# Rotary embedding in an attention stage: the swap as an f32 matmul, the projection copied out by ScalarE, cosine on GpSimd, sine on VectorE

## The reference

```python
def _rotate_half(x):
    x1, x2 = jnp.split(x, 2, axis=-1)
    return jnp.concatenate([-x2, x1], axis=-1)

def _apply_rope(x, cos, sin):
    return x * cos + _rotate_half(x) * sin

q = (x @ Wq).reshape(Bd, Sd, H, DH + D_ROPE)        # x: (4, 512, 256), H = 16, DH = 16, D_ROPE = 64
q_nope, q_rope = (q[..., :DH], q[..., DH:])
c_kv = x @ Wdkv
kv = (c_kv @ Wukv).reshape(Bd, Sd, H, 2 * DH)
k_rope = x @ Wkr
q_rope = _apply_rope(q_rope, cos, sin)
k_rope = _apply_rope(k_rope, cos, sin)
scores = einsum(q_nope, k_nope) + einsum(q_rope, k_rope)
attn = softmax(where(causal, scores * scale, -1e9))
out = einsum(attn, v).reshape(Bd, Sd, H * DH) @ Wo
```

## Time and profile before

| | us |
|---|---|
| median of three runs | 1441.34 |
| lowest, highest | 1438.83, 1446.45 |
| the profiled execution | 1443.96 |
| its span, first to last instruction | 1442.2 |

### The profile page before, as it was taken

How to read it: one execution, slowest core, us unless ns; L and a number is a source line. 1 busy time by engine, 2 the same in 40 slices (tenths; PEclk the granted TensorE clock), 3 DMA queues, 4 the chain that set the end, 5 groups by cost and what they waited for, 6 DMA issues and landing times. The chain is left out here.

```text
span 1442.2 us, 32153 instructions
## 1 busy us (share of the span) xinstructions
PE 1169.6 (81%) x12288; PEld 881.9 (61%) x12288; DVE 985.1 (68%) x2082; ACT 647.3 (45%) x1519; POOL 599.3 (42%) x525
## 2 busy tenths in 40 slices
PE   2789898998874599998817885998999648999992
PEld 1356566665653398987713553665766527989882
DVE  6479798887786556456565956788797574555554
ACT  4367566666564133333446653353333223333342
POOL 0245445545430234334300195688696213333220
PEclk9899999999995599999958998999999759999996
DMA  4655756656533598876240002000000039966635
GB/s 158 155 131 157 175 167 172 167 164 158 147 111 87 197 419 345 277 248 252 66 173 8 15 25 45 16 17 2 2 2 2 27 93 397 419 238 243 253 99 186
DMA packets 98186, 216.83 MB, mean 150 GB/s; under 512 B 28977, under 2 KB 68146, under 8 KB 91890
## 3 DMA queue, kind: packets, MB, share of 16 engines
q1 hardware_dynamic: 88434, 192.22, 41.0%
q0 software_dynamic: 7488, 20.46, 4.2%
q10 hardware_dynamic: 2112, 2.10, 0.4%
HBM read 157.40 MB, written 40.04 MB: 137 GB/s over the span
## 5 line engine op out<-in xcount | busy, mean ns | idle before, releaser
L1228 ACT ACTIVATE ffn_h<-ffn_bank,ffn_b 128x256 f32<-128x256 f32 (+1 forms) x384 | 143.9, 431 | 278.5 <-PE ffn_bank L118 259.3
L1407 DVE CAST ffn_hh<-ffn_h 128x512 f16<-128x512 f32 (+1 forms) x192 | 80.7, 420 | 182.8 <-ACT ffn_h L1228 166.5
L116 PE MATMUL ffn_bank<-ffn_hh,ffn_W 128*128 128x256 f16 (+1 forms) x768 | 181.0, 254 | 8.9 <-DVE ffn_hl L1409 8.9
L1042 POOL DMA_INDIRECT ffn_xs<-xn_rows,ffn_from_rows x78 | 79.4, 1019 | 244.4 <-PE ffn_bank L1123 158.2
L118 PE MATMUL ffn_bank<-ffn_hh,ffn_W 128*128 128x256 f16 (+1 forms) x768 | 180.8, 254 | 0.0
L117 PE MATMUL ffn_bank<-ffn_hl,ffn_W 128*128 128x256 f16 (+1 forms) x768 | 180.7, 253 | 0.0
L644 ACT ACTIVATE att_prob<-att_bank,att_nmax 128x512 f32<-128x512 f32 (+3 forms) x256 | 127.1, 525 | 31.3 <-DVE att_nmax L726 30.0
L733 DVE TENSOR_TENSOR att_ptl<-att_bank,att_pth 128x384 f16<-128x384 f32 (+1 forms) x192 | 113.9, 593 | 34.4 <-ACT att_pth L651 34.4
L651 ACT ACTIVATE att_pth<-att_bank 128x384 f16<-128x384 f32 (+1 forms) x192 | 101.3, 528 | 79.0 <-PE att_bank L591 79.0
L1049 POOL DMA_INDIRECT y_rows<-ffn_y,ffn_to_rows x78 | 77.4, 993 | 133.6 <-DVE ffn_y L1418 86.9
L591 PE MATMUL att_bank<-main_identf,att_prob 128*128 128x128 f32 x640 | 99.6, 281 | 35.7 <-ACT att_prob L644 19.6
(11 more groups left out here) (345 smaller groups left out, 3222.6 us busy)
## 6 DMA issues: line engine op xcount, KB each, us to landing
ffn_W<-split_w SPq DMA_DIRECT2D x46, 2048.0 KB, 19.3
att_piece<-in_ffn_w SPq DMA_DIRECT2D x32, 512.0 KB, 5.2
split_w<-att_halves SPq DMA_DIRECT2D x32, 512.0 KB, 4.2
att_Q<-att_pair SPq DMA_DIRECT2D x64, 128.0 KB, 2.4
ffn_back<-y_rows SPq DMA_DIRECT2D x16, 512.0 KB, 9.1
att_KB<-att_krl SPq DMA_DIRECT2D x8, 512.0 KB, 5.6
att_Q<-att_pair SPq DMA_DIRECT2D x64, 64.0 KB, 2.1
xn_rows<-ffn_XN SPq DMA_DIRECT2D x8, 512.0 KB, 2.6
```

What stands on the lines that cost most here:

```text
L116: pe.matmul(out, ah, bh, start=start, stop=False)
L1228: ins_ = act.activation(h[layer][:, m, 0:n], bank[1 + 2 * layer + u][:, (m % 2) * n:(m % 2 + 1) * n], ACT.Gelu, bias=bias[:, ds(e + m, 1)])
```

## The change

The swapped weights `wt`, and the swapped columns of `wx`, are gone. A job's first half is as before. Its second half is two f32 matmuls on `turned`: a signed swap matrix (`swap`, made once by DVE from the identity) times the sine product, and the identity times the cosine product, added in bank 1. The products are now made from a copy `raw` of the projection in SBUF: ACT makes the copy, POOL the cosine product, DVE the sine product. ACT then reads bank 1 twice, for the f16 high part and for the f32 `rope`, from which POOL makes the low part as before. POOL's sum is gone. In the start, each job's first half is put ahead of the second half of the job before it.

```diff
+            def turn_half(job):
+                at = turn[job] % 2
+                pe.wait_ge(swap_made, 2)
+                pe.wait_ge(sin_done, turn[job] + 1)
+                pe.matmul(bank[1][:, :], swap[:, :], turned[:, at, 1, :], start=True, stop=False)
+                pe.wait_ge(cos_done, turn[job] + 1)
+                return pe.matmul(bank[1][:, :], identf[:, :], turned[:, at, 0, :], start=False, stop=True)
...
-                if what == "pair":
-                    ins = project(bank[1][:, :], wth, wtl, n % (NH // 2) * P, P, n // (NH // 2))
-                elif what == "kr":
-                    ins = project(bank[1][:, :], wxh, wxl, KT_AT, P, n)
+                if what in ("pair", "kr"):
+                    ins = turn_half(job)
...
-            for job in START:
-                first_half(job)
+            first_half(START[0])
+            for job, following in zip(START, START[1:] + [None]):
+                first_half(following)
                 second_half(job)
...
+            def copy_raw(job):
+                what, n = job
+                r = turn[job]
+                act.wait_ge(first_ready, nth[job] + 1)
+                if r >= 2:
+                    act.wait_ge(second_ready, nth_second[ropes[r - 2]] + 1)
+                act.activation(raw[:, r % 2, :], bank[0][:, :], ACT.Copy, scale=ATT_SCALE if what == "kr" else 1.0).then_inc(first_drained, 1)
...
-                act.wait_ge(summed, r + 1)
+                act.wait_ge(second_ready, nth_second[job] + 1)
...
-                    ins = act.activation(pair[:, n % 2, 0, :], rope[:, r % 2, :], ACT.Copy)
+                    ins = act.activation(pair[:, n % 2, 0, :], bank[1][:, :], ACT.Copy)
                 ins.then_inc(rope_high, 1)
+                if r >= 2:
+                    act.wait_ge(rope_low, r - 1)
+                act.activation(rope[:, r % 2, :], bank[1][:, :], ACT.Copy).then_inc(second_drained, 1)
...
+                if what in ("pair", "kr"):
+                    r = turn[job]
+                    dve.wait_ge(first_drained, nth[job] + 1)
+                    if r >= 2:
+                        dve.wait_ge(second_ready, nth_second[ropes[r - 2]] + 1)
+                    dve.tensor_tensor(turned[:, r % 2, 1, :], raw[:, r % 2, :], sinT[:, :], ALU.mult).then_inc(sin_done, 1)
+                    return
...
-                pool.tensor_tensor(rope[:, r % 2, :], turned[:, r % 2, 0, :], turned[:, r % 2, 1, :], ALU.add).then_inc(summed, 1)
+                    wait_alone(pool, second_ready, nth_second[ropes[r - 2]] + 1, passed)
+                pool.tensor_tensor(turned[:, r % 2, 0, :], raw[:, r % 2, :], cosT[:, :], ALU.mult).then_inc(cos_done, 1)
...
                 if last:
-                    sum_rope(last)
                     low_rope(last)
+                if job_at(g):
+                    cosine(job_at(g))
                 if g % 2 == 0:
                     high_piece(g // 2)
                     low_piece(g // 2)
```

More of the change, by code:

```diff
@@ L318, in attention_stage @@
         turned, rope = t.sb("turned", [P, 2, 2, S]), t.sb("rope", [P, 2, S])
-        pair = t.sb("pair", [P, 2, 2, S], F16)
+        pair, swap = t.sb("pair", [P, 2, 2, S], F16), t.sb("swap", [P, P])
+        raw = t.sb("raw", [P, 2, S])
         qnh, qnl, knh, knl = (t.sb(n, [P, 2, S], F16) for n in ("qnh", "qnl", "knh", "knl"))
@@ L367, in attention_stage @@
         nth_second = {job: n for n, job in enumerate(j for j in done if j[0] != "lat")}
-        turn = {job: n for n, job in enumerate(j for j in done if j[0] in ("pair", "kr"))}
+        ropes = [j for j in done if j[0] in ("pair", "kr")]
+        turn = {job: n for n, job in enumerate(ropes)}
         def wait_drained(eng, job):
@@ L655, in high_half @@
                 what, n = job
+                if what in ("pair", "kr"):
+                    high_rope(job) if x else copy_raw(job)
+                    return
                 if what not in ("lat", "qn", "kn", "v", "oT") or (what == "lat" and x):
@@ L693, in _ @@
                 high_half(job, 1)
-                high_rope(job)
             probs(0, 0)
@@ L717, in _ @@
         def _(dve):
+            halves_of = lambda a: a[:, :].rearrange("p (b x r) -> p b x r", x=2, r=HALF)
+            for x in range(2):
+                dve.tensor_scalar(halves_of(swap)[:, :, x, :], halves_of(identf)[:, :, 1 - x, :], -1.0, None, ALU.mult).then_inc(swap_made, 1)
             dve.memset(zeros[:, :], 0.0).then_inc(zeros_made, 1)
@@ L755, in drain @@
                 what, n = job
-                if what == "lat" and x:
+                if what in ("lat", "pair", "kr") and x:
                     return
-                if what in ("pair", "kr", "op"):
+                if what in ("pair", "kr"):
+                    r = turn[job]
[3 more added lines that the diff above has]
+                    dve.tensor_tensor(turned[:, r % 2, 1, :], raw[:, r % 2, :], sinT[:, :], ALU.mult).then_inc(sin_done, 1)
+                    return
+                if what == "op":
                     if x == 0:
@@ L826, in _, with cosine @@
         def _(pool):
-            def sum_rope(job):
+            def cosine(job):
                 what, n = job
@@ L843, in low_rope @@
                 wait_alone(pool, rope_high, r + 1, passed)
+                wait_alone(pool, second_drained, nth_second[job] + 1, passed)
                 if what == "kr":
@@ L864, in _ @@
             for job in START:
-                sum_rope(job)
+                cosine(job)
                 low_rope(job)
```

37 lines of the change are left out of this document (10 added, 27 removed).

## The result

| | before | after |
|---|---|---|
| median of four runs each, us | 1442.08 | 1563.57 |
| lowest, highest | 1438.83, 1446.45 | 1560.83, 1565.35 |
| span of the profiled execution | 1442.2 | 1563.6 |

The change makes the kernel slower by 121.5 us: a ratio of 1.084, interval 1.081 to 1.087. The direction was forecast, the size was not: 1478, with a range up to 1502.

What follows compares the result with a forecast made beforehand. PE and DVE were both taken as near their limit, so hand-overs count. Span 1442.2 + 30 (loop) + 2 (start) + 5 (clock) = 1479.2, put at 1478 us after adjusting from profiled span to median; range 1450 to 1502.

Steps and rivals of the forecast that it cites:

- Fewer weights: Before attention: the split of wt goes and wx shrinks, so attention starts about 2.4 us earlier.
- The chain up to the cosine: Even head: ACT's copy runs 115.62 to 116.22, POOL's cosine 116.40 to 117.67, and DVE's normalising product stands until 117.75.
- The rival without a lock: Even head: the sine runs beside the cosine, interval 11.84 us, kernel 1450 us; chance 0.15.
- The sine: Even head: DVE's sine product of 0.67 us follows the held normalising product and ends at about 118.36, not 117.69.
- The f32 matmul: PE, second half: 0.43 us each, two 0.86 against 1.29 for six fp16 matmuls; 15.5 us less PE work in all.
- The rival at four steps: PE, second half: each f32 job's half ends 0.86 us later, 26 us in all, kernel 1504 us; chance 0.03.
- The odd head: ACT's two copies ahead of chunk 1 make an odd head 5.67 us instead of 5.51, 0.15 more.
- The clock: Loop: low clock behind PE's new 1.7 us waits, +5 us net, ends 0 and +30.
- The rival by the clock: Loop: the clock falls at every PE wait, 36 us instead of 5, kernel 1509 us; chance 0.13.
- The start: Start of attention: later latent copy and longer key chain; +2 us with layer norm, ends 0 and +4.
- A gain taken for the change's: Loop: ACT's wait for POOL's sum, 20.8 us in 27 times, goes away; part of why intervals average 11.60, not 11.09.
- the interval of 11.09: Loop before the change: two heads between POOL's pair sums at 110.34 and 121.43; with +1.28 and +0.15 it becomes 12.52 us.

Runs made afterwards that it cites:

- piece_odd: The changed kernel with POOL's two passes over an expert piece moved from the even heads to the odd ones: 1548.28 us, 1.072 of the kernel before.
- sine_psum: The changed kernel with the sine product read from PSUM bank 0, still behind the normalising product: 1522.42 us, 1.058 of the kernel before.
- f16_swap: The changed kernel with the two products, swap matrix and identity of the second half in f16: 1518.91 us, 1.052 of the kernel before.
- sine_ahead: The changed kernel with the sine product read from PSUM bank 0 and placed ahead of the normalising product: 1491.65 us, 1.034 of the kernel before.
- start_order: The kernel before with only the new order of PE at the start of attention: 1455.20 us, 1.007 of the kernel before.
- old_start: The changed kernel with PE's order at the start of attention as it was before: 1555.28 us, 1.076 of the kernel before.
- f16_old_start: The changed kernel with f16 second-half matmuls, the sine from PSUM ahead of the normalising product, and the old start order: 1424.64 us, 0.991 of before.
- rope_last: The kernel before with ACT's high half of the rope sum moved behind the next head's second softmax piece: 1436.48 us, 0.994 of the kernel before.
- no_cosine: The changed kernel without POOL's cosine product, the identity matmul taking the raw copy: 1514.39 us, 1.049 of the kernel before.

## Why the prediction was wrong

By its own steps, on the head shown above:

- **Fewer weights: right.** -2.0 us against -2.4.
- **The chain up to the cosine: right.** Copy 3.19 and cosine 3.97 us behind the head's first transposes were forecast, 3.17 and 4.06 measured. The normalising product stands until 0.09 behind the cosine, as forecast. The rival without a lock is out.
- **The sine: the step that failed most.** "The sine product of 0.67" was taken to run once the cosine had ended. The prediction named what is queued behind the wait on DVE and on PE, but not what is queued behind the cosine on POOL: the cast, without a pause. At the cosine's end the normalising product is served, the cast has begun, and the sine has to wait for it (piece_odd and sine_psum show it). With that the sine took 1.52, and the swap starts 7.00 us into the head and not 6.00. 30 x 1.00 = 30 us.
- **The f32 matmul: mis-sized by half.** "Four such f32 matmuls ... 1.88" read the "x4" of the earlier trace rows as matmuls. It counts records, and an f32 matmul has two, so the row is two matmuls of 0.86. The job costs 1.72 instead of 0.86, more than the 1.29 of the six it replaces: PE loses 15.5 us where I let it gain as much. 30 x 0.86 = 26 us. The rival at four steps, to which I gave 0.03 against the page FP8 and Floating Point Precision of the Trainium skill (TensorE Precision Notes, 4 passes for true fp32), was the true case; f16_swap's trace agrees with the page, one fourth of the step in f16. The row never spoke against it.
- **The odd head: right.** 5.67 was forecast. The interval 133.66 to 148.86 less 9.38 leaves 5.82: 30 x 0.15 = 5 us.
- **The clock: too small.** Swap and identity are 1.72 of work by the steps and take 2.38 in the head shown (136.60 to 138.98), because the second half of them is at the low level behind the wait, like the 0.63 of L589 at 140.47: 0.66 a head, 20 us, where 5 was taken. The heads differ widely. Of the loop's 33 halves 14 take 1.79 or 1.80, the full clock, and 12 take 3.2 to 3.6, as here:

```profile
151.80 2.04 PE L516 MATMUL att_bank<-att_turned,att_swap 128*128 128x512 f32 x2 [2.31 <-DVE att_turned L786]
153.64 1.63 PE L518 MATMUL att_bank<-att_turned,main_identf 128*128 128x512 f32 x2
```

  The mean is 2.48, so that over all of them it is 25 us and not 20. The length of the wait alone does not decide: waits of 2.18 us had both outcomes (93.15 and 108.27), the three of 3.10 the slow one. In sine_ahead, with waits of 0.73 in the mean, none of the 33 takes over 1.8. The rival by the clock thus held in part.
- **The start: wrong cause and size.** +9.2 to the scores instead of +2. I had priced the latent's copies coming later, not the bank that every first half shares (start_order). With the old order it is +2.5 (old_start) although the stage begins 2.0 us earlier, so the chain of the keys and pairs costs some 4.5 by itself, where 2 was taken. The f32 matmuls and the held-off sine are in that: with f16 and the early sine the scores begin at 60.1 (f16_old_start).
- **A gain taken for the change's:** ACT's wait for the sum is worth 8 us (rope_last). It was counted inside the interval of 11.09, about rightly, and is not part of the miss.

Sum: 1478 + 30 + 26 + 5 + (20 - 5) + (9 - 2) = 1561, against 1563.6 measured. With the 25 of all halves it would be 1566. The terms are worked out from one head, whose interval (15.20) is a little under the mean (15.43) and whose clock fell half-way, so their closeness to the total is partly luck; the three large ones have a run each: the sine and its clock 72 us (sine_ahead), the matmul 45 (f16_swap, which takes away 1.29 a job and not the missing 0.86), the start 8 to 12 (old_start; 6.7 of scores in its trace). What of the 72 is wait and what is clock no run separates; by the head it is 1.71 and 0.66 of 2.37, times 30 = 71, and by all 33 halves of the two traces 53 and 23.

## What to carry to other kernels

Before two engines that exclude each other on SBUF share a chain, list what each has queued behind the shared step: when the waiting instruction has been served, the next one behind it can find the other engine's next step already begun. Put the product that others wait for ahead of small SBUF products, and let one operand come from PSUM. An order that fills a wait must be checked against the buffer it needs: a "next job first" order on one bank is no overlap. Divide a profile's busy time by instructions of the code, not by records.

## What the runs showed of the hardware

- Two DVE products of two SBUF tensors, one behind the other, against two POOL instructions with no gap between them: the first ends 0.09 us behind POOL's first, the second is held off until POOL's second has ended (0.68 becomes 1.52 us, 29 pairs). Where POOL pauses 0.18 us the sine gets in (no_cosine), and POOL's next pass takes 2.48 instead of 2.13.
- A single product that had waited through one POOL instruction was once held off by the next as well (2.58 us) and once served ahead of it (1.35), each the same way in three traces.
- The size of the product doesn't matter: 128x512 is blocked like 128x64. With one operand in PSUM it is not blocked (0.68 beside cosine and cast).
- An f32 matmul of 512 columns has two records of 0.43, 0.86 in all, against 0.21 in f16.
- A new order of PE's work of the same amount came with six more us of waits ahead of the first matmuls of the projections and a granted clock of 0.79 instead of 0.89 in 33 to 65 us, and cost 11 us by the medians. That clock alone doesn't set the start: f16_old_start has 0.71 there, and its scores begin at 60.1 us.
